# Wide loop of a decoder layer: value and output products two in a step, the inverse root earlier and one round shorter, loads and weight splits in another order

## The reference

```python
x = layernorm(x + attn(x))           # three attentions, below
x = layernorm(x + xattn(x, ctx))     # 154 keys, scores with a distance bias
x = layernorm(x + ffn(x))            # 8 experts, 2 per token, and a shared one
```

```python
ctx = softmax(modulated scores) @ v                    # 16 heads of 16
causal_ctx = mha(x, x, ca_Win, ..., ca_Wout, heads=4)  # 4 heads of 64
ctx = ctx * (1.0 - CAUSAL_W) + causal_ctx * CAUSAL_W
meta_ctx = mha(ctx, ctx, mc_Win, ..., mc_Wout, heads=4)  # 4 heads of 64
ctx = ctx * (1.0 - META_W) + meta_ctx * META_W
return ctx @ Wo + bo
# layernorm(y) = (y - mean(y)) / sqrt(var(y) + 1e-5)
```

## Time and profile before

| | us |
|---|---|
| Median of three runs (3252.2 to 3260.85) | 3252.91 |
| The profiled execution | 3290.99 |
| Its span, first to last instruction | 3289.3 |
| Mean granted clock of TensorE | 0.917 |

### The profile page before, as it was taken

The page is one execution under the profiler, slowest core; times in us unless marked ns, Lnnn a source line. Parts: engine busy times, 40 slices in busy tenths (PEclk is TensorE's granted clock), DMA queues, the critical chain, the costliest instruction groups (busy, mean ns, idle before and its releaser), DMA issues. The chain is left out here.

```text
span 3289.3 us, 45964 instructions
## 1 busy us (share of the span) xinstructions
PE 2791.9 (85%) x14080; PEld 1814.9 (55%) x14081; DVE 2081.8 (63%) x3082; ACT 1402.5 (43%) x2432; POOL 997.4 (30%) x978
## 2 busy tenths in 40 slices
PE   7959999999999699999989886488886553999996
PEld 6834445545444345555645443366564433888885
DVE  5558877777774688888878875445544841433346
ACT  2305666666667244444444442223333210233335
POOL 4565530000000164444455544510000126133322
PEclk9969999999999799999999998689987776999998
DMA  6899973534530635565544422665663222213424
GB/s 234 306 224 297 261 192 52 78 53 65 73 48 11 144 105 167 146 171 147 167 123 121 122 81 80 146 74 87 88 86 86 69 108 88 95 55 131 169 93 130
DMA packets 243973, 409.06 MB, mean 124 GB/s; under 512 B 38687, under 2 KB 139143, under 8 KB 242503
## 3 DMA queue, kind: packets, MB, share of 16 engines
q1 hardware_dynamic: 190807, 274.58, 35.5%
q0 software_dynamic: 23712, 79.14, 7.1%
q10 hardware_dynamic: 29264, 52.96, 6.2%
HBM read 231.46 MB, written 175.12 MB: 124 GB/s over the span
## 5 line engine op out<-in xcount | busy, mean ns | idle before, releaser
L624 DVE TENSOR_REDUCE an_m<-an_psm 128x1 f32<-128x1024 f32 x512 | 604.6, 1220 | 188.7 <-PE an_psm L548 187.5
L604 ACT ACTIVATE an_probs<-an_pst 128x512 f32<-128x512 f32 x1024 | 533.1, 603 | 257.9 <-PE an_pst L575 257.5
L1356 ACT ACTIVATE wj_probs<-wj_pst 128x512 f32<-128x512 f32 x512 | 301.7, 597 | 376.6 <-PE wj_pst L1208 363.3
L548 PE MATMUL an_psm<-an_ks,an_qs 127*128 127x512 f32 x1024 | 366.7, 442 | 40.8 <-POOL an_ks L499 31.1
L1087 POOL TENSOR_TENSOR wj_sums<-wj_sums,wj_probs 128x512 f32<-128x512 f32 x192 | 276.4, 1440 | 341.8 <-ACT wj_probs L1356 338.9
L575 PE MATMUL an_pst<-an_qs,an_ks 128*128 128x512 f32 x1024 | 337.1, 407 | 10.5 <-issue 5.9
L1383 DVE TENSOR_REDUCE wj_m<-wj_pm 128x1 f32<-128x512 f32 x512 | 325.2, 680 | 29.4 <-PE wj_pm L1183 29.1
L548 PEld LDWEIGHTS an_psm<-an_ks,an_qs 127*128 127x128 f32 x1024 | 179.9, 198 | 275.5 <-issue 172.7
L560 PE MATMUL an_pacc<-an_probs,an_vs 128*32 128x512 f32 x2048 | 273.4, 606 | 11.3 <-ACT an_probs L604 11.0
L575 PEld LDWEIGHTS an_pst<-an_qs,an_ks 128*128 128x128 f32 x1024 | 192.7, 189 | 121.5 <-ACT an_probs L604 70.0
L1197 PE MATMUL wj_pacc<-wj_probs,wj_vs 128*64 128x512 f32 x1024 | 250.9, 611 | 0.0
(11 more groups left out here) (396 smaller groups left out, 5550.0 us busy)
## 6 DMA issues: line engine op xcount, KB each, us to landing
ew_w<-scr_ws SPq DMA_DIRECT2D x10, 3072.0 KB, 13.5
scr_ws<-an_wpair POOLq DMA_DIRECT2D x27, 1024.0 KB, 5.6
an_qs<-scr_q SPq DMA_DIRECT2D x64, 256.0 KB
an_ks<-scr_k SPq DMA_DIRECT2D x64, 256.0 KB
ac_qs<-scr_xq SPq DMA_DIRECT2D x64, 256.0 KB, 7.6
wj_qs<-scr_mq ACTq DMA_DIRECT2D x24, 512.0 KB, 5.4
wj_ks<-scr_mk ACTq DMA_DIRECT2D x24, 512.0 KB, 5.8
scr_xs<-an_blank POOLq DMA_DIRECT2D x18, 516.0 KB, 25.9
```

What stands on the lines that cost most here:

```text
L548: last = pe.matmul(psm[:, n % 2, kh], qs[0:MROW, slot, j, q0:q0 + P], ks[0:MROW, slot, j, kh * CH:(kh + 1) * CH], start=True, stop=True)
L604: act.activation(probs[:, s % 2, j], pst[:, (GH * s + j) % RING], ACT.Exp, scale=HD ** -0.5).then_inc(exp_done, 1)
L624: dve.tensor_reduce(m1[:, hq, col:col + 1], psm[:, n % 2], AX.XY, ALU.max).then_inc(mx_done, 1)
L1356: act.activation(probs[:, x % RING, j], pst[:, j], ACT.Exp, scale=BHD ** -0.5).then_inc(exp_done, 1)
```

## The change

- The table: joint and norm `mix` one step on, joint `query` one on, joint `value` two in a step (14, 14, 15, 15); norm `wide` one on, `out` two in a step (10, 10, 11, 11), norm `query` one on.
- `slopes` does three rounds instead of four (14 instructions) and stands at x - 1 instead of x - 2. The first guess and the rounds are the same, so 1/sqrt is a little less exact.
- The six weight pieces of the norm chunks are split in the order mc_Wout, Wo (step 2), then the scaled xattn_Wq (step 4), and the products wait for as many pieces as they need.
- The second loads of group 1 and the first loads of group 2, and the values of both, are issued by ScalarE in group 0 instead of by SP ahead of `joint_weights`.
- At the end SP prepares the last norm chunk before it stores the queries of chunk 5.

```diff
@@ -781,8 +781,8 @@
                 return NSTEP * (c + 2)
             return NSTEP * (c + 2 + NKIND) if c < NCH - 1 else NSTEP * (NCH + NKIND) + LAG
 
-        JOINT = dict(wide=(2, 2), narrow=(3, 3), mix=(5, 6), query=(9, 10, 11, 12), value=(13, 14, 15, 16))
-        NORM = dict(wide=(2, 2), mix=(5, 6), out=(9, 10, 11, 12), turn=(16, 17), query=(19, 20))
+        JOINT = dict(wide=(2, 2), narrow=(3, 3), mix=(6, 7), query=(10, 11, 12, 13), value=(14, 14, 15, 15))
+        NORM = dict(wide=(3, 3), mix=(6, 7), out=(10, 10, 11, 11), turn=(16, 17), query=(20, 21))
         work = {}
         for c in range(NCH):
             for kind, plan in (("joint", JOINT), ("norm", NORM)):
@@ -1010,10 +1010,6 @@
             max_row(0, 0)
             load_first(1)
             max_row(0, 1)
-            load_second(1)
-            loadv(sp, 1)
-            load_first(2)
-            loadv(sp, 2)
             joint_weights()
             for G in range(NGR):
                 if G:
@@ -1051,10 +1047,10 @@
                     max_row(G + 1, 1)
             store(BLOCKS - 1)
             load_residual(NCH - 2)
+            prepare("norm", NCH - 1)
+            load_residual(NCH - 1)
             for n in range(KH):
                 store_query("norm", NCH - 3, n)
-            prepare("norm", NCH - 1)
-            load_residual(NCH - 1)
             store_norm(NCH - 2)
             for c in (NCH - 2, NCH - 1):
                 for n in range(KH):
@@ -1115,7 +1111,7 @@
                     pool.wait_ge(x1_done, NT * c)
                 link(pool.tensor_scalar(ve[:], mv[:, :, 1], EPS, None, ALU.add))
                 link(pool.tensor_scalar(rstd[:].bitcast(I32), ve[:].bitcast(I32), -0.5, float(0x5f3759df), ALU.mult, ALU.add))
-                for _ in range(4):
+                for _ in range(3):
                     link(pool.tensor_tensor(half[:], rstd[:], rstd[:], ALU.mult))
                     link(pool.tensor_tensor(half[:], half[:], ve[:], ALU.mult))
                     link(pool.tensor_scalar(half[:], half[:], -0.5, 1.5, ALU.mult, ALU.add))
@@ -1145,19 +1141,19 @@
                     pool.wait_ge(w_in, 32 + 48)
                     pool.wait_ge(pg_ready, past("joint", "value", NCH - 1, NT - 1))
                     for n in range(2 * KH):
-                        if n >= KH:
-                            scaled = raw_weights(3 * H)[:, n % KH, Q0:Q0 + H]
-                            pool.tensor_scalar(scaled, scaled, HD ** -0.5, None, ALU.mult).then_inc(w_scaled, 1)
-                            pool.wait_ge(w_scaled, n % KH + 1)
-                        split_weights(8 + n, raw_weights(3 * H), (W0, Q0)[n // KH], n % KH)
+                        split_weights(8 + n, raw_weights(3 * H), (W0, Y0)[n // KH], n % KH)
                 if x == begin("norm", 0) + 4:
                     for n in range(KH):
-                        split_weights(12 + n, raw_weights(3 * H), Y0, n)
+                        scaled = raw_weights(3 * H)[:, n, Q0:Q0 + H]
+                        pool.tensor_scalar(scaled, scaled, HD ** -0.5, None, ALU.mult).then_inc(w_scaled, 1)
+                        pool.wait_ge(w_scaled, n + 1)
+                        split_weights(12 + n, raw_weights(3 * H), Q0, n)
+                for kind, what, c, n in at(x - 1):
+                    if what == "out" and n == NT - 1:
+                        slopes(c)
                 for kind, what, c, n in at(x - 2):
                     i = number(kind, c)
                     u = buffers(kind, c)
-                    if what == "out" and n == NT - 1:
-                        slopes(c)
                     if what == "mix":
 
                         pool.wait_ge(za_done, KH * i + n + 1)
@@ -1244,7 +1240,7 @@
                 elif what == "narrow":
                     pe.matmul(dst, sel[:, n], rs[:], start=True, stop=True).then_inc(pg_ready, 1)
                 elif what == "mix":
-                    pe.wait_ge(w_lo, 8 if kind == "joint" else 12)
+                    pe.wait_ge(w_lo, 8 if kind == "joint" else 10)
                     pe.wait_ge(cnb_done, KH * i + KH)
                     mm3(pe, dst, [cols(0, x, W0 + n * P) for x in range(KH)], [cols(1, x, W0 + n * P) for x in range(KH)],
                         [b.cna[:, x] for x in range(KH)], [b.cnb[:, x] for x in range(KH)]).then_inc(pg_ready, 1)
@@ -1252,13 +1248,14 @@
                     if kind == "joint":
                         pe.wait_ge(zb_done, KH * i + KH)
                     else:
+                        pe.wait_ge(w_lo, 14)
                         pe.wait_ge(pg_free, past("norm", "turn", c, KH - 1))
                     xa, xb = (za, zb) if kind == "joint" else turned(c)
                     mm3(pe, dst, [cols(0, x, Q0 + n * P) for x in range(KH)], [cols(1, x, Q0 + n * P) for x in range(KH)],
                         [xa[:, x] for x in range(KH)], [xb[:, x] for x in range(KH)]).then_inc(pg_ready, 1)
                 elif what in ("value", "out"):
                     if what == "out":
-                        pe.wait_ge(w_lo, 14)
+                        pe.wait_ge(w_lo, 12)
                         pe.wait_ge(zb_done, KH * i + KH)
                     first = V0 if what == "value" else Y0
                     tok = slice(n * P, (n + 1) * P)
@@ -1360,9 +1357,11 @@
                     if G and s == 2:
 
                         act.wait_ge(pv_done, NSTEP * G)
-                    if G and s in (2, 4) and G + 1 < NGR:
+                    if x == 1:
+                        loadv(act, 1)
+                    if s in (2, 4) and G + 1 < NGR:
                         load1(act, G + 1, s // 2 - 1)
-                    if G and G + 2 < NGR:
+                    if G + 2 < NGR:
                         if s == 6:
                             needs(act, G + 2)
                         if s in (6, 8, 10, 12):
```

## The result

The kernel after takes 3238.97 us (median of 6 runs, 3234.68 to 3243.78) against 3258.81 us of the kernel before (median of 6 runs, the three on record with the prediction among them): ratio 0.9939, 95% interval 0.9919 to 0.9959. It is faster, by 20 us and not by 58, and its time lies 19 us above the upper end of the range. The profiled execution took 3240.91 us.

What follows compares the result with a forecast made beforehand. TensorE was taken to set the pace almost everywhere, so only its stalls and low clock pay. Gains of 15 + 6 + 4 + 5 + 11 + 17 = 58 us off the median of 3252.91 gave 3195 us, range 3168 to 3220.

Steps and rivals of the forecast that it cites:

- Part 3, joint groups: Joint groups 2 to 9: mix one step on covers a 0.6 us wait in each of eight groups, -5 us.
- pairs wait for their evictions: Rival, 14 groups: paired products fill both buffers and wait for VectorE's late evictions, 3275 us; chance 0.04.
- Part 1, middle norm groups: Groups 11 to 14: earlier, shorter chain frees the transposes, a maxima wait replaces them; 60.2 to 56.5 us each, -15.
- The last norm group: Group 15, without maxima to wait for: first transposes come about 3.5 us earlier, less low clock, -6 us.
- Part 2, group 10: First norm group: mix product waits only for the weight pieces it needs, 57.2 to about 53 us, -4.
- Part 4, the start: Group 0: loads moved to ScalarE let weights start earlier, TensorE's 8.27 us wait and low clock go, -11 us.
- moved loads collide: Rival, start: loads share the same engines whichever queue issues them, 2.5 us of 8.27 stay, 3199 us; chance 0.10.
- Part 5, the tail: Behind the last scores: transposes -4, denominators' wait -3, earlier chain and normalising -11, partly hiding each other, -17 us.

Runs made afterwards that it cites:

- e1: The kernel before, unedited, profiled a second time: 3252.50 us, ratio 0.9990.
- e4: Kernel after with the load of the next chunk's denominators issued before the third query block's store instead of behind the fourth: 3217.78 us, ratio 0.9872.
- e3: Kernel after with the joint groups' mixing and query steps put back as before, value products still two in a step: 3212.38 us, ratio 0.9868.
- e12: Kernel before with only three rounds for four and the chain issued one step on instead of two: 3230.88 us, ratio 0.9940.
- e6: Kernel after with the joint mixing and query steps and the whole norm table of before put back, value pairs kept: 3219.68 us, ratio 0.9882.

## Why the prediction was wrong

The forecast was 58 us and the change brought 20. Measured against e1's profile, whose stage fits the timed difference, my parts came to: groups 0 and 1 -5.8, joint +19.2, group 10 -4.9, groups 11 to 14 -12.4, last part -16.4; in all -20. (The first profile of before has a stage 13.6 us shorter, so single parts are uncertain by some us; where I compare with it, I say so.)

- **Part 3, joint groups, failed**: -5 forecast, +19 measured (+26 against the first profile, whose joint groups were the shorter ones). The step that failed is the sentence that the eviction before a pair's second product is one "for which VectorE, idle for 54.2 - 46.0 = 8.2 us of a joint group, should be in time". It took idle time of a whole group as slack at one place, where VectorE in fact stood 3.4 us for the denominators and TensorE 2.4 us for it. I also moved the query products without counting what their stores carry behind them on SyncE: the load of the next denominators, whose reader stayed at step 14. The sum of a group agrees: 2.4 us of wait, and 0.02 x 57.5 = 1.2 us of clock (0.98 over the eight groups, 1.00 before), less the 0.6 us wait that went, are 3.0 of the 3.2 us. e4 puts that load ahead and the loss is gone; e3 leaves it where it was and it is not there either. The rival "pairs wait for their evictions" named the wait that TensorE shows, at 0.04, but for a wrong reason (maxima and a sum in front) and for all 14 groups. The norm groups' pairs wait for nothing of the kind. Even without the transfer, the mixing moved on gives next to nothing: e4's joint groups (54.4 us for 3 to 8) are as long as e3's (54.6) with the 0.6 us wait in them; a wait for the split reciprocals is there instead.
- **Part 1, middle norm groups**: -15 forecast, -8.8 against the first profile and -12.4 against e1's. The mechanism came as written: normalising 4.5 us (4.0 forecast), three sums beside it, transposes free, and in their place 4.3 us for the maxima buffer (4 forecast). The mis-sized term is the clock: I had it at full, and it is 0.96, that is 0.04 x 58.0 = 2.3 us, so 51.6 + 4.3 + 2.3 = 58.2 for 58.0 measured. TensorE stood 4.3 us, and the first product of 512 columns behind that took 0.79 us, where one at full clock takes 0.40. e12 shows that three rounds and the earlier issue are the whole of it (57.2 us); the new norm table with its output pairs, which I counted as what brings the chain forward, adds nothing here (e6).
- **The last norm group**: -4.0 against the first profile (52.6 to 48.6), forecast -6.
- **Part 2, group 10**: -3.5 and -4.9 by the profile compared with; forecast -4. Right.
- **Part 4, the start**: -6.3 by the means of all profiles (-5.8 against e1's), for -11. GpSimd's wait fell as stepped, 20.0 to 6.0. What I left out is that the splits then run beside VectorE's sums and reciprocals, so 2.5 of the 8.3 us of hole came back as a wait for maxima. The rival "moved loads collide" gave the size better (-7), even its 2.5 us that stay, but by luck, since its cause is not what the rows show: the small transfers had landed when GpSimd went on at 1138.68, within the 1142 of the forecast.
- **Part 5, the tail**: 78.7 to 66.0 against the first profile, -12.7 for -17, inside its bounds. The denominators' wait went, and chunk 6's normalising took 2.46 us for 5.44, with 1.4 us of wait for its transposes instead of 10.4. What I had not seen is a wait of 2.6 us for chunk 6's split reciprocals; and the first transposes still waited 2.1 us, the last 4.0 for 6.2. TensorE and VectorE in the tail of the kernel after, against the earlier trace rows:

```profile
2003.78 0.63 PE L1268 MATMUL wj_pg<-all_ident,wj_x 128*128 128x128 f32 x4 [2.05 <-DVE wj_x L1461]
...
2009.11 0.71 PE L1239 MATMUL wj_pg<-wj_rs,wj_sel 128*128 128x512 f32 x2 [2.56 <-DMA wj_rs<-scr_rwide]
...
2036.34 2.46 DVE L1461 TENSOR_SCALAR wj_x<-wj_x,wj_mv,wj_rstd 128x256 f32<-128x256 f32 x4 [0.35 <-POOLq L1119]
...
2038.94 1.16 PE L1268 MATMUL wj_pg<-all_ident,wj_x 128*128 128x128 f32 x8 [1.36 <-DVE wj_x L1461]
```

Together, by e1's profile: 24 of the 38 us that were missing lie in the joint groups, 5 at the start, 7 in the last part, 3 in the middle groups; group 10 gave 1 more than forecast.

## What to carry to other kernels

When a product is moved by a step, follow its result past the eviction: the store that reads it, and every load queued behind that store whose reader does not move. An engine that is idle a seventh of the time can still stand, in order, behind one late transfer, with the evictions of the critical engine behind it. And take a second profile of the kernel before when one is longer than its own median: the price of a stretch was off by 1 us a group, and one stage by 46 us.
